# Embedding, attention, state and sign layers for 64 sequences on one core: xn1's turn ahead of the key projection

## The chip, the cores and the metric

The program runs on one core of a Trainium2 chip. The metric is the device time in microseconds (us) of one execution. Of the kernel before there are three timed runs and one profiled execution.

## The reference, cut to what matters

For 64 sequences of 128 token ids, each with 256 features:

```python
x = emb[inp]                                   # [64, 128, 256]
q, k, v = x @ Wq.T + bq, x @ Wk.T + bk, x @ Wv.T + bv     # 16 heads of 16
attn = softmax(q k^T / 4); h = (attn v) @ Wo.T + bo
n = layernorm(h)
gate = sigmoid(n @ gate_w.T + gate_b)
state = exclusive_scan(decay, (n @ B_w.T) @ C_w.T)        # over the 128 tokens
h = h + gate * state
h = h + layernorm(h) @ sign(weight).T
```

## The kernel before, in words

Two sequences make a pair, so there are 32 pairs. The function `turns` runs 38 turns, t from -2 to 35; a hardware loop holds those from 6 to 29. A turn is a software pipeline: in turn t the attention of pair t is computed, the queries and keys of pair t + 1 are made, and the rest of the layer runs for pairs t - 1 to t - 4. Each engine has its own `turn` function, in which the order of its instructions is written out by hand; semaphores order the engines among each other (`await_event`), and no scheduler moves anything.

The attention of a pair has 8 steps, s = 0 to 7, four heads of one sequence each. In TensorE's `attention(s)` (L730) stand:

- `turn_probs(s)`: four transposes of the probabilities of step s - 2 into `ps_t` (L695);
- `scores(s)`: two products into `ps_s` (L683);
- `context(s)`: eight narrow products of step s - 3 into the bank `ps_c` (L712). For s = 3 this is step 0 of pair t, and it waits until ScalarE has moved the second half of pair t - 1 out of `ps_c` (`move_ctx`, L357, tile `ctx_raw`).

All of TensorE's products share line 623, and all copies through `move_block` on ScalarE share L364, so the tiles tell them apart. A projection is made of float32 operands split in a high and a low part: ScalarE casts the high part out of a PSUM bank (`xTh`, `xn1Th`), VectorE subtracts it from the same bank for the low part (`xTl`, `xn1Tl`, L494, `low_features`), and TensorE multiplies high by high, high by low and low by high.

Around the change a turn goes so:

- TensorE after `attention(2)`: the prefix sums of pair t - 3 (`earlier` by `state_in` into bank g3, L753), the transposes of the embeddings of pair t + 1 into g0 (`to_features`, L758, tile `x_emb`), `attention(3)`, the context rows of pair t - 1 into g2 (L720), the key projection of pair t + 1 into g1 (L766, 12 products), which waits for `xTl`, and the transposes of the normed `xn1` of pair t - 2 into g3 (L770), which wait until the bank g3 has been read.
- ScalarE in steps 2 and 3: `move_probsT(2)` (L347), the copy `xTh` (L374), the copy `ctx_raw` (L375), the exponentials of step 2 (L338), `move_probsT(3)`, the exponentials of step 3.
- VectorE in step 2: the maxima of the scores (L486), `v_aug` (L567), `xTl` (L572), the two halves of `xn1` (`norm_apply`, L519), `gated` (L578), which reads the sums out of g3, and `h1` (L583), which adds `h0`.

GpSimd issues the gathers of the embeddings (L277) and computes the inverse square roots of the layer norms (L286, L291). SyncE spreads keys and queries over partitions with 12 transfers per pair, into `k_stack` and `q_stack`, which the scores of the next turn read.

Of the kernel before, what the change touches and what calls it, by code (L numbers as in the profile page):

```python
# [52 lines left out]
def build(nc, x, emb, wqT, bq, wkT, bk, wvT, bv, woT, bo, b_w, c_wT, gate_wT, gate_b, log_decay, ffn_wT, out):  # L53
    ctx = ExitStack()
    with ctx:
# [60 lines left out]
        xn1, xn2 = sb("xn1", [P, 2, D]), sb("xn2", [P, 2, D])  # L116
# [55 lines left out]
        def exists(pair):  # L172

            return not isinstance(pair, int) or 0 <= pair < PAIRS

        def await_event(eng, semaphore, per, pair, nth):

            if exists(pair):
                eng.wait_ge(semaphore, pair * per + nth)
# [120 lines left out]
        def _(act):  # L300
# [29 lines left out]
            def turn(t, par):  # L330
                def exponentials(s):

                    if exists(t):
                        await_event(act, dve_max, STEPS, t, s + 1)
                        p2, s2 = before(t, s, 2)
                        await_event(act, pe_pT, STEPS, p2, s2 + 1)
                        for j in range(HPS):
                            last = nc.scalar.activation(probs[s % 2][:, j], ps_s[s % 2][:, j * SEQ:j * SEQ + SEQ],  # L338
                                                        ACT.Exp, bias=neg_max[s % 2][:, j:j + 1])
                        last.then_inc(act_exp, 1)  # L340
# [18 lines left out]
                def move_block(pair, dst, src, filled, freed, done):  # L359

                    if exists(pair):
                        await_event(act, filled, 1, pair, 1)
                        await_event(act, freed, 1, pair - 1, 1)
                        nc.scalar.copy(dst[:], src[:]).then_inc(done, 1)  # L364
# [6 lines left out]
                exponentials(1)  # L371

                move_probsT(2)
                move_block(t + 1, xT[0], g0, pe_x, pe_v, act_x)  # L374
                move_ctx(t - 1, 1)  # L375
                exponentials(2)

                move_probsT(3)
                exponentials(3)
# [39 lines left out]
        def _(dve):  # L419
# [59 lines left out]
            def turn(t, par):  # L479
# [84 lines left out]
                if exists(t):  # L564
# [4 lines left out]
                        g2[:].rearrange("p (b h w) -> p b h w", b=2, w=HD),  # L569
                        bv_row[:].rearrange("p (h w) -> p h w", w=HD).unsqueeze(1).to_broadcast([P, 2, HEADS, HD]),  # L570
                        ALU.add).then_inc(dve_v, 1)
                low_features(t + 1, xT, g0, act_x, pe_v, dve_xlo)  # L572
                if exists(t - 2):
                    norm_apply(t - 2, h0[par], mv1, rs1, xn1, rs1_done, pe_xn1T, dve_xn1)
                if exists(t - 3):
                    await_event(dve, pe_sums, 1, t - 3, 1)
                    await_event(dve, act_tanh, 1, t - 3, 1)
                    nc.vector.scalar_tensor_tensor(gated[:], gate_tanh[:], 1.0,  # L578
                                                   g3[:].rearrange("p (b d) -> p b d", b=2), ALU.add,
                                                   ALU.mult).then_inc(dve_gated, 1)  # L580
                    await_event(dve, dve_gated, 1, t - 3, 1)
                    await_event(dve, dve_y, 1, t - 4, 1)
                    nc.vector.tensor_tensor(h1[:], gated[:], h0[1 - par][:], ALU.add).then_inc(dve_h1, 1)  # L583
# [37 lines left out]
        def _(pe):  # L621
# [53 lines left out]
            def turn(t, par):  # L675
# [84 lines left out]
                if exists(t - 1):  # L760
                    await_first((dve_v, 1, t, 1), (dve_h0, 1, t - 2, 1))
                    context_rows(1, g2)
                if exists(t + 1):
                    await_event(pe, dve_xlo, 1, t + 1, 1)
                    await_first((dve_ctx, 2, t - 1, 1), (dve_klo, C, t, C))
                    feature_major(g1, wk, xT, pe_k)  # L766
                if exists(t - 2):
                    await_event(pe, dve_xn1, 2, t - 2, 2)
                    await_event(pe, dve_h1, 1, t - 3, 1)
                    to_features(g3, lambda b: xn1[:, b], pe_xn1T)  # L770

                attention(4)
                if exists(t + 1):
# [59 lines left out]
```

## Time and profile before

| | us |
|---|---|
| median of 3 runs | 828.27 |
| lowest, highest | 826.53, 829.21 |
| the profiled execution | 829.6 |
| its span | 827.5 |
| TensorE busy, weight loads | 755.6, 644.6 |
| VectorE busy | 584.8 |
| ScalarE busy | 582.0 |
| GpSimd busy | 130.5 |

The profiled execution is 1.3 us above the median. Busy times of TensorE overlap in part, since its products are pipelined; what it does in a stretch is read from the starts of its instructions. The mean granted clock of TensorE is 0.98 of full speed; it is below it in the first and the last few slices alone.

### The profile page before, as it was taken

What the parts mean: (1) busy time and instruction counts of PE and PEld (TensorE: products, weight loads), DVE (VectorE), ACT (ScalarE), POOL (GpSimd) and SP (SyncE); (2) the same over time, 40 slices, a digit from 0 to 9 for tenths busy, and PEclk for the clock granted to TensorE, in tenths of its full rate; (3) what the DMA queues carried; (4) which work ended last, traced back from release to release, by engine and by line L of the source; (5) the groups of instructions that cost most, each with busy time, mean ns of one, the idle gap of its engine ahead of it and who ended that gap; (6) DMA issues with size and microseconds to landing.
All of it is one profiled execution on the core that took longest, in us unless ns stands there. A gap on an engine that the chain in (4) does not pass through costs nothing.

```text
span 827.5 us, 21122 instructions
## 1 busy us (share of the span) xinstructions
PE 755.6 (91%) x7047; PEld 644.6 (78%) x7047; DVE 584.8 (71%) x1307; ACT 582.0 (70%) x1643; POOL 130.5 (16%) x205
## 2 busy tenths in 40 slices
PE   1389999999999999999999999999999999999964
PEld 0377888888888888888888888888888888888754
DVE  5345677777777777777777787777777777777763
ACT  2177877777777777777777777777877777778710
POOL 7210111111110111111101111111011111100010
PEclk9889999999999999999999999999999999999986
DMA  4222223123322321233223322332233222322000
GB/s 129 89 90 78 90 91 97 52 85 103 100 91 89 101 94 59 75 101 101 89 89 101 101 56 73 98 101 90 88 101 101 61 73 94 101 90 90 15 14 25
DMA packets 56015, 69.67 MB, mean 84 GB/s; under 512 B 6768, under 2 KB 41648, under 8 KB 55984
## 3 DMA queue, kind: packets, MB, share of 16 engines
q1 hardware_dynamic: 52048, 60.48, 21.3%
q0 software_dynamic: 3072, 8.39, 4.9%
q10 hardware_dynamic: 864, 0.40, 0.2%
q8 instruction: 18, 0.29, 0.2%
q14 instruction: 13, 0.11, 0.0%
HBM read 10.52 MB, written 8.39 MB: 23 GB/s over the span
## 4 chain that ended last, share of the span: by engine, by line
PE 76%; issue 13%; ACT 3%; DVE 2%; DMA 2%; SPq 2%; POOL 1%; ACTq 1%; POOLq 0%; DVEq 0%
PE ps_g L623 39%; PE ps_t L695 11%; PE ps_c L623 10%; PE ps_g L672 7%; PE ps_s L623 6%; PE ps_g L720 4%; ACT ctx_raw L357 2%; SPq L234 1%; DMA q_stack<-q_low 1%; DVE raw L452 1%; DMA gb_row<-in_gate_b 1%; SPq L239 0%; POOL rs L286 0%; DMA raw<-in_woT 0%; POOL rs L291 0%
## 5 line engine op out<-in xcount | busy, mean ns | idle before, releaser
L338 ACT ACTIVATE probs<-ps_s,neg_max 128x128 f32<-128x128 f32 x1024 | 299.6, 400 | 73.0 <-DVE neg_max L486 72.9
L486 DVE TENSOR_REDUCE neg_max<-ps_s 128x4 f32<-128x512 f32 x256 | 176.4, 689 | 155.2 <-PE ps_s L623 132.7
L347 ACT COPY probsT<-ps_t 128x512 f32<-128x512 f32 x256 | 155.5, 608 | 63.7 <-PE ps_t L695 54.2
L695 PE MATMUL ps_t<-ident,probs 128*128 128x128 f32 x1024 | 154.7, 274 | 3.9 <-ACT probsT L347 3.9
L623 PE MATMUL ps_s<-k_stack,q_stack 128*128 128x256 f32 x512 | 124.2, 325 | 7.8 <-DMA q_stack<-q_low 7.8
L623 PE MATMUL ps_c<-probsT,v_aug 128*32 128x128 f32 x2048 | 109.3, 285 | 16.6 <-ACT ctx_raw L357 16.1
L695 PEld LDWEIGHTS ps_t<-ident,probs 128*128 128x128 f32 x1024 | 120.0, 142 | 5.6 <-ACT probs L338 3.3
L286 POOL TENSOR_TENSOR rs<-ve,neg_half 128x2 f32<-128x2 f32 x32 | 22.2, 693 | 449.4 <-DVE ve L513 449.4
L623 PEld LDWEIGHTS ps_s<-k_stack,q_stack 128*128 128x128 f32 x512 | 78.1, 193 | 8.8 <-DMA q_stack<-q_low 8.7
L623 PEld LDWEIGHTS ps_c<-probsT,v_aug 128*32 128x32 f32 x2048 | 40.5, 108 | 53.3 <-ACT ctx_raw L357 17.5
L277 POOL DMA_INDIRECT x_emb<-in_emb,id_col x64 | 64.5, 1008 | 37.5 <-PE ps_g L672 21.7
L364 ACT CAST xTh<-ps_g 128x512 fp32r<-128x512 f32 x32 | 18.8, 586 | 56.0 <-PE ps_g L672 56.0
L291 POOL TENSOR_TENSOR rs<-ve,neg_half 128x2 f32<-128x2 f32 x32 | 22.8, 714 | 197.7 <-DVE ve L513 197.7
L501 DVE BATCH_NORM_STATS2 stats<-h 128x6 f32<-128x256 f32 x128 | 47.9, 416 | 1.2
L672 PE MATMUL ps_g<-ident,xn 128*128 128x128 f32 x256 | 39.6, 278 | 9.4 <-DVE h L583 5.0
L494 DVE TENSOR_TENSOR xTl<-ps_g,xTh 128x512 fp32r<-128x512 f32 x32 | 22.2, 693 | 36.5 <-ACT xTh L364 36.5
L519 DVE TENSOR_SCALAR xn<-h,mv,rs 128x256 f32<-128x256 f32 x128 | 46.6, 406 | 1.8 <-POOL rs L286 1.0
L623 PE MATMUL ps_g<-wgh,xn1Th 128*128 128x256 f32 x128 | 39.8, 311 | 1.4 <-DVE xn1Tl L494 1.4
L623 PE MATMUL ps_g<-xTh,wkh 128*128 128x256 f32 x128 | 39.3, 307 | 1.7 <-DVE xTl L494 1.7
L720 PE MATMUL ps_g<-ident,ctx_raw 128*128 128x128 f32 x256 | 40.4, 281 | 0.0
L623 PE MATMUL ps_g<-wvh,xTh 128*128 128x256 f32 x128 | 40.0, 312 | 0.0
L623 PE MATMUL ps_g<-wsh,xn1Th 128*128 128x256 f32 x128 | 39.7, 310 | 0.0
(120 smaller groups left out, 1829.1 us busy)
## 6 DMA issues: line engine op xcount, KB each, us to landing
k_stack<-k_high SPq DMA_DIRECT2D x128, 128.0 KB, 2.4
q_stack<-q_high SPq DMA_DIRECT2D x64, 256.0 KB, 2.5
k_stack<-k_low SPq DMA_DIRECT2D x64, 128.0 KB, 2.3
q_stack<-q_low SPq DMA_DIRECT2D x32, 256.0 KB, 2.5
out<-y SPq DMA_DIRECT2D x32, 256.0 KB
x_emb<-in_emb,id_col POOLq DMA_INDIRECT x64, 3.6
raw<-in_wkT SPq DMA_DIRECT2D x1, 256.0 KB, 3.1
raw<-in_wqT SPq DMA_DIRECT2D x1, 256.0 KB, 4.2
```

What stands on the lines that cost most here:

```text
L277: nc.gpsimd.indirect_dma_start(x_emb[par][b][:], None, emb, bass.IndirectOffsetOnAxis(ap=id_col[par][b][:], axis=0)).then_inc(gathered[par ...
L286: nc.gpsimd.tensor_tensor(rs1[:], ve1[:], neg_half[:], ALU.pow).then_inc(rs1_done, 1)
L291: nc.gpsimd.tensor_tensor(rs2[:], ve2[:], neg_half[:], ALU.pow).then_inc(rs2_done, 1)
L338: last = nc.scalar.activation(probs[s % 2][:, j], ps_s[s % 2][:, j * SEQ:j * SEQ + SEQ], ACT.Exp, bias=neg_max[s % 2][:, j:j + 1])
L347: nc.scalar.copy(probsT[st % 2][:], ps_t[:]).then_inc(act_pT, 1)
L486: nc.vector.tensor_reduce(neg_max[s % 2][:], ps_s[s % 2][:].rearrange("p (h k) -> p h k", h=HPS), axis=AX.X, op=ALU.max, negate=True).then ...
L501: nc.vector.bn_stats(stats[:, b], h[:, b]).then_inc(done_st, 1)
L519: nc.vector.tensor_scalar(xn[:, b], h[:, b], mv[:, b, 0:1], rs[:, b:b + 1], ALU.subtract, ALU.mult).then_inc(done, 1)
L623: return nc.tensor.matmul(dst, lhsT, rhs, start=first, stop=last)
L672: last = nc.tensor.transpose(dst[:, at:at + SEQ], src(b)[:, c * P:c * P + P], ident[:])
L695: last = nc.tensor.transpose(ps_t[:, j * SEQ:j * SEQ + SEQ], probs[st % 2][:, j], ident[:])
L720: last = nc.tensor.transpose(dst[:, g * P:g * P + P], ctx_raw[b][:, g], ident[:])
```

## The change

Three engines get another order in steps 2 and 3, and one wait becomes another:

- ScalarE copies the contexts and computes the exponentials of step 2 before it copies the embeddings.
- VectorE forms `xn1` and `gated` before it forms `xTl`; `h1` follows `xTl`.
- TensorE turns `xn1` before the key projection, and waits there for `gated` in place of `h1`.

The diff:

```diff
@@ ScalarE
                 move_probsT(2)
-                move_block(t + 1, xT[0], g0, pe_x, pe_v, act_x)
                 move_ctx(t - 1, 1)
                 exponentials(2)
+                move_block(t + 1, xT[0], g0, pe_x, pe_v, act_x)
@@ VectorE
-                low_features(t + 1, xT, g0, act_x, pe_v, dve_xlo)
                 if exists(t - 2):
                     norm_apply(t - 2, h0[par], mv1, rs1, xn1, rs1_done, pe_xn1T, dve_xn1)
                 if exists(t - 3):
...
                     nc.vector.scalar_tensor_tensor(gated[:], gate_tanh[:], 1.0,
                                                    g3[:].rearrange("p (b d) -> p b d", b=2), ALU.add,
                                                    ALU.mult).then_inc(dve_gated, 1)
+                low_features(t + 1, xT, g0, act_x, pe_v, dve_xlo)
+                if exists(t - 3):
                     await_event(dve, dve_gated, 1, t - 3, 1)
                     await_event(dve, dve_y, 1, t - 4, 1)
                     nc.vector.tensor_tensor(h1[:], gated[:], h0[1 - par][:], ALU.add).then_inc(dve_h1, 1)
@@ TensorE
                     context_rows(1, g2)
+                if exists(t - 2):
+                    await_event(pe, dve_xn1, 2, t - 2, 2)
+                    await_event(pe, dve_gated, 1, t - 3, 1)
+                    to_features(g3, lambda b: xn1[:, b], pe_xn1T)
                 if exists(t + 1):
                     await_event(pe, dve_xlo, 1, t + 1, 1)
                     await_first((dve_ctx, 2, t - 1, 1), (dve_klo, C, t, C))
                     feature_major(g1, wk, xT, pe_k)
-                if exists(t - 2):
-                    await_event(pe, dve_xn1, 2, t - 2, 2)
-                    await_event(pe, dve_h1, 1, t - 3, 1)
-                    to_features(g3, lambda b: xn1[:, b], pe_xn1T)
```

ScalarE in the middle of a turn of the filled pipeline, before: `probsT` is `move_probsT`, `probs` the exponentials, `xTh` the high part of the embeddings.

```order
L347 COPY probsT<-ps_t 128x512
L364 CAST xTh<-ps_g 128x512
L357 COPY ctx_raw<-ps_c 128x512
L338 ACTIVATE probs<-ps_s,neg_max 128x128 x4
L347 COPY probsT<-ps_t 128x512
```

And now, in the same place:

```order
L347 COPY probsT<-ps_t 128x512
L357 COPY ctx_raw<-ps_c 128x512
L338 ACTIVATE probs<-ps_s,neg_max 128x128 x4
L364 CAST xTh<-ps_g 128x512
L347 COPY probsT<-ps_t 128x512
```

The copy of the contexts no longer stands behind the copy of the embeddings, and that copy stands behind four exponentials more.

VectorE in step 2 and at the start of step 3 of such a turn, before; `neg_max` is the maxima, the `h` behind `gated` is `h1`.

```order
L494 TENSOR_TENSOR xTl<-ps_g,xTh 128x512
L519 TENSOR_SCALAR xn<-h,mv,rs 128x256 x2
L578 SCALAR_TENSOR_TENSOR gated<-gate_tanh,ps_g 128x512
L583 TENSOR_TENSOR h<-gated,h 128x512
L179 REGISTER_ALU
L486 TENSOR_REDUCE neg_max<-ps_s 128x4
```

And now (one line more stands in the file from here on, so L583 has become L584); the two halves of `xn` stand right ahead of this piece:

```order
L577 SCALAR_TENSOR_TENSOR gated<-gate_tanh,ps_g 128x512
L179 REGISTER_ALU
L494 TENSOR_TENSOR xTl<-ps_g,xTh 128x512
L584 TENSOR_TENSOR h<-gated,h 128x512
L179 REGISTER_ALU
L486 TENSOR_REDUCE neg_max<-ps_s 128x4
```

`xTl` has moved behind three instructions that do not need it, and its place ahead of `h1` and the maxima is kept.

## Rows read from the trace of the kernel before

**Rows 1.** The page, part 1: busy time, share of the span and instructions by engine.

```profile
PE 755.6 (91%) x7047; PEld 644.6 (78%) x7047; DVE 584.8 (71%) x1307; ACT 582.0 (70%) x1643; POOL 130.5 (16%) x205
```

**Rows 2.** Who waited for whom: us in total, times, longest us.

```profile
PE ps_c L623 <- ACT ctx_raw L357: 16.1, 30, 0.6
```

**Rows 3.** Timeline, TensorE, one turn: start, us, instruction, idle before and its releaser.

```profile
412.56 0.43 PE L623 MATMUL ps_c<-probsT,v_aug 128*32 128x128 f32 x8
412.92 1.12 PE L623 MATMUL ps_g<-state_in,earlier 128*128 128x512 f32 x2
413.88 0.60 PE L672 MATMUL ps_g<-ident,x_emb 128*128 128x128 f32 x4
...
414.68 0.48 PE L623 MATMUL ps_s<-k_stack,q_stack 128*128 128x256 f32 x2
415.72 0.42 PE L623 MATMUL ps_c<-probsT,v_aug 128*32 128x128 f32 x8 [0.56 <-ACT ctx_raw L357]
416.08 0.66 PE L720 MATMUL ps_g<-ident,ctx_raw 128*128 128x128 f32 x4
416.49 0.36 PE L623 MATMUL ps_g<-xTh,wkh 128*128 128x256 f32 x1
...
418.01 0.63 PE L672 MATMUL ps_g<-ident,xn 128*128 128x128 f32 x4
418.48 0.60 PE L695 MATMUL ps_t<-ident,probs 128*128 128x128 f32 x4
```

**Rows 4.** Timeline, ScalarE, the same turn.

```profile
414.59 0.59 ACT L364 CAST xTh<-ps_g 128x512 fp32r<-128x512 f32 x1 [1.57 <-PE ps_g L672]
415.07 0.59 ACT L357 COPY ctx_raw<-ps_c 128x512 f32<-128x512 f32 x1
415.55 1.16 ACT L338 ACTIVATE probs<-ps_s,neg_max 128x128 f32<-128x128 f32 x4
416.56 0.63 ACT L347 COPY probsT<-ps_t 128x512 f32<-128x512 f32 x1
```

**Rows 5.** Timeline, VectorE, the same turn.

```profile
412.67 0.69 DVE L486 TENSOR_REDUCE neg_max<-ps_s 128x4 f32<-128x512 f32 x1 [0.85 <-ACT probs L338]
413.28 0.68 DVE L567 TENSOR_TENSOR v_aug<-ps_g,bv_row 128x512 f32<-128x512 f32 x1
415.21 0.69 DVE L494 TENSOR_TENSOR xTl<-ps_g,xTh 128x512 fp32r<-128x512 f32 x1 [1.25 <-ACT xTh L364]
415.82 0.73 DVE L519 TENSOR_SCALAR xn<-h,mv,rs 128x256 f32<-128x256 f32 x2
416.46 0.68 DVE L578 SCALAR_TENSOR_TENSOR gated<-gate_tanh,ps_g 128x512 f32<-128x512 f32 x1
...
417.78 0.68 DVE L486 TENSOR_REDUCE neg_max<-ps_s 128x4 f32<-128x512 f32 x1
```

**Rows 6.** Timeline, TensorE, turn 31, the last with an attention: scores and context of step 3.

```profile
767.92 0.48 PE L623 MATMUL ps_s<-k_stack,q_stack 128*128 128x256 f32 x2
768.33 0.43 PE L623 MATMUL ps_c<-probsT,v_aug 128*32 128x128 f32 x8
```

**Rows 7.** Timeline, turn 0 on VectorE and TensorE, and the start of turn 1's scores.

```profile
45.44 0.69 DVE L486 TENSOR_REDUCE neg_max<-ps_s 128x4 f32<-128x512 f32 x1 [2.98 <-PE ps_s L623]
...
47.66 0.39 PE L623 MATMUL ps_g<-xTh,wkh 128*128 128x256 f32 x1 [0.19 <-DVE xTl L494]
...
59.01 0.50 PE L623 MATMUL ps_s<-k_stack,q_stack 128*128 128x256 f32 x2 [0.91 <-DMA q_stack<-q_low]
```

**Rows 8.** Timeline, GpSimd, the turn of rows 3: the second gather's issue.

```profile
413.55 0.95 POOL L277 DMA_INDIRECT x_emb<-in_emb,id_col  x1 [0.30 <-issue]
```

**Rows 9.** The turn's last transfer to a stack, its landing (page, part 6), the next scores.

```profile
426.57 0.61 SPq L239 DMA_DIRECT2D q_stack<-q_low  x1
...
q_stack<-q_low SPq DMA_DIRECT2D x32, 256.0 KB, 2.5
...
430.50 0.48 PE L623 MATMUL ps_s<-k_stack,q_stack 128*128 128x256 f32 x2
```

## The prediction

> **What bounds the kernel now.** I read the page first, then who waited for whom, then the timelines of one turn, engine by engine. The page shows TensorE busy for 91% of the span and VectorE and ScalarE for 71% and 70% [rows 1]. So TensorE is the engine to follow, and a change of order that adds and removes no instruction can only win what TensorE waits. In the filled pipeline the view of waits has one wait of TensorE that comes back: its context products wait for the copy `ctx_raw`, 30 times, 16.1 us in total, never over 0.6 us [rows 2]. There are 30 turns in which both that copy and the copy of the embeddings exist, turns 1 to 30.
>
> The timeline says why. ScalarE waits 1.57 us with the copy `xTh` until TensorE has turned the embeddings, and the copy `ctx_raw`, which needs only products that ended at 412.99, stands in the queue behind it: it starts at 415.07 and TensorE goes on at 415.72 [rows 3, 4]. The exponentials of step 2 stand there too; their maxima were ready at 413.36 [rows 5], they start at 415.55.
>
> How much is the wait worth? Its row says 0.56 us of idle time. Starts say more: from the scores of step 3 to their context products it is 1.04 us here [rows 3]. Turn 31 has no embeddings to copy and so is a turn of this kernel without that block: there it is 0.41 us [rows 6]. I take the difference, **0.63 us** per turn, because TensorE's time is the distance of starts. The idle time of the waits' row, 16.1 / 30 = 0.54 us, is the low bound.
>
> **The change, part by part.** I lay the new order over the turn of rows 3 to 5, on its own clock.
>
> *ScalarE.* The copy `ctx_raw` can start when the context products of step 2 have ended, 412.99, say 413.06. A copy takes its place for 0.48 us (415.07 to 415.55) and four exponentials for 1.01 us (415.55 to 416.56) [rows 4]. So the exponentials start at 413.54, behind maxima that ended at 413.36, and ScalarE is free at 414.55. The transposes of the embeddings end at 414.48, and `xTh` started 0.11 us later, at 414.59 [rows 3, 4]. It starts at 414.59 again: the four exponentials just fit in what was idle time, with 0.04 us to spare. This is the tightest fit of the sum, though nothing is lost at once if it fails (below).
>
> *VectorE.* After `v_aug` (start 413.28) the next place is 413.88 with the distance of 0.61 us that follows such an instruction (415.21 to 415.82). `xn` goes there and takes 0.64 us, `gated` starts at 414.52. It needs the prefix sums, whose products end at 414.04 [rows 3], and ends at 415.20. `xTl` needs `xTh`, which ends at 415.18, and starts at 415.21 as before, ending at 415.90. `h1` at 415.82 and the maxima of step 3 at 416.43 follow, the latter 1.35 us earlier than now [rows 5].
>
> *TensorE.* Context products of step 3 at 414.68 + 0.41 = 415.09 (`ctx_raw` has ended at 413.65), context rows at 415.45, the turn of `xn` at 415.86, with the distances of 0.36 and 0.41 us in rows 3. It needs `gated`: ended at 415.20, 0.66 us to spare. Had the wait stayed on `h1` (416.51) it would have cost 0.7 us; this is what the new wait is for. The turn takes 0.47 us, so the key projection starts at 416.33 and needs `xTl`: ended at 415.90, 0.43 us to spare. It takes 1.52 us (416.49 to 418.01), and step 4 begins at 417.85 in place of 418.48 [rows 3]. Nothing of the 0.63 us is lost here. The move of the projection behind the transposes costs nothing by itself, as the same groups stand there with the same lengths.
>
> *What is late next.* Behind step 4 everything that ScalarE and VectorE do is released by TensorE or by the maxima of step 3, which move by 1.35 us, so all keeps its distance to TensorE or gains. The transfers: the last one for the stack is issued at 426.57 and lands 2.5 us later, at 429.07; the scores that need it start at 430.50 [rows 9]. That is 1.43 us of cover, and 0.80 us are left even if no transfer moves. SyncE's queue keeps its order, and it starts behind the high part of the keys, which comes earlier. GpSimd gets nothing new.
>
> *The turns that do not profit.* Before turn 3 there are no prefix sums. They fill 0.96 us (412.92 to 413.88) [rows 3], and it is in these that the exponentials of step 2 find room. Count from the start of the context products of step 2. Without sums the old order has the embeddings' transposes at +0.36, `xTh` at +1.07, `ctx_raw` at +1.55, step 3's context products at +2.20 and the key projection at +2.97. The new one has `ctx_raw` at +0.50, exponentials at +0.98, `xTh` at +1.99, `xTl` at +2.61 to +3.30, and the projection at +3.34. Turn 1 loses 0.37 us. In turn 2 the turn of `xn`, 0.47 us, moves ahead and fills the gap: it gains 0.10 us. In turn 0 there is no `ctx_raw`: the maxima of step 2 end at 46.13, the exponentials leave at 47.18, `xTl` ends at 48.49, and the projection starts at 48.53 in place of 47.66 [rows 7]. These 0.87 us go on through the keys and the transfers to the scores of turn 1, which already wait for the stack. In the last turns TensorE waits for a chain through VectorE in which nothing moves; I put them at zero, within 0.2 us.
>
> **The sum:** turns 3 to 30 win 28 x 0.63 = 17.6 us, turn 2 0.1; turns 0 and 1 cost 0.87 + 0.37 = 1.2. That is **-16.5 us**. Against the profiled execution's own 829.6 it gives 813.1; that execution is 1.3 us above the median of the runs, and against the median, 828.27, it gives **811.8 us**. By the low bound (28 x 0.54, less 1.1) it would be -14.0 and 814.3; by the longest idle time of that row, 0.6, with the 0.07 on top that starts show over idle time here, it is 28 x 0.67 - 1.1 = 17.7, and 810.6. With 1.4 us for the spread of three runs the forecast's own range is 809.2 to 815.7.
>
> **The rivals.**
>
> *VectorE and GpSimd get in each other's way.* `xn` moves from 415.82 to 413.88, into the issue of the second gather, which runs from 413.55 to 414.50 [rows 8]. If `xn` had to wait for its end, it would start at 414.50, `gated` at 415.14, `xTl` at 415.75 and end at 416.44. The projection would start at 416.48, 0.15 us late, and a turn would win 0.48 us: 28 x 0.48 - 1.1 = 12.3, or **816.0 us**. Against it: two `xn` of 256 elements take 0.64 us and one `v_aug` of 512 takes 0.61 us [rows 5], so `xn` shows no faster way of reading that could need more ports than `v_aug` does. The Trainium skill, in "SBUF — State Buffer", section "Who interferes with whom", states that VectorE and GpSimd share one pair of ports, that a tensor_scalar in a two-port mode takes it for its whole length, and that whichever comes second is blocked; `xn` is a tensor_scalar. By that rule, were `xn` in such a mode, the time would be the 816 of this rival; outside it the page sees no conflict. Chance 0.08.
>
> *Another wait takes the gap.* The stack's landing is the nearest: 1.43 us of cover, of which the gain takes 0.63. If the transfers landed 1.4 us later than the row's 2.5, the whole gain would become a wait for `q_stack`, and the time would stay at **828**. Against it: the transfers begin earlier than now. That the change is without effect, for the queues being in truth in another order, is as good as excluded, as the orders above are written out by hand. Together 0.06.
>
> *Slower: the exponentials in front of the copy of the embeddings.* The place is ScalarE at 414.55. If they leave later than 415.02, the key projection waits for `xTl`; from 415.65 on (1.06 us late: 0.43 to spare and the 0.63 won) the turn is longer than before, since also keys, transfers and step 4 wait. Turns 0 and 1 show that this can happen. If all turns lost what turn 1 loses, it would be 28 x 0.37 + 1.1 = 11.5 us more, **839.8 us**. For it: only 0.04 us between the two. Against it: it takes a full us, and what precedes (maxima at 412.67, context products at 412.56) is released by TensorE itself in each turn. Chance 0.06.
>
> **How the numbers follow.** The forecast has 0.80, the ports 0.08, no gain 0.06, slower 0.06. Faster by over 0.3% (2.5 us, about what a measurement of this kernel can tell from no change) are the first two, 0.88; within it 0.06; slower 0.06. The range reaches from the forecast's low end, 809.2, to the ports' case and 1 us of spread, 817.0.
>
> **What the profile after should show.** The wait of `ps_c` for `ctx_raw` is gone from the list, and the distance from the scores to the context products of step 3 is 0.41 us in all turns. `ctx_raw` starts about 0.5 us behind the context products of step 2, the exponentials next, `xTh` right at the end of the embeddings' transposes. A turn is 0.63 us shorter than before. TensorE does not wait for `gated`, and for `xTl` only in turns 0 to 2. `xn` still takes 0.64 us and starts 0.6 us behind `v_aug`. A row of TensorE waiting for `xTl` in every turn would speak for the ports if `xn` starts late, and for the last rival if `xTh` does; a row for `q_stack` in every turn for the other. Were the distance 0.41 and the turn still as long, my reading of the turn would be wrong.

## The result, and the profile after

The changed kernel took **808.64 us** (median of four runs, 808.38 to 809.01), beside 828.24 us for the kernel before (826.53 to 829.21). The ratio is 0.9766, with a 95% interval of 0.9749 to 0.9783. It was timed twice more, beside other experiments: 810.33 us each time, with 827.82 and 827.43 us for the kernel before, ratios 0.9792 (0.9773 to 0.9810) and 0.9791 (0.9773 to 0.9809). So the gain is 17 to 20 us. The forecast was 811.8 us, a gain of 16.5; the first measurement lies 0.6 us below the low end of its range, 809.2, and the other two lie inside it.

The page, part 1, of the kernel after. Instructions and busy times have hardly changed [rows 1]; the span is 20.7 us shorter than 827.5.

```profile
span 806.8 us, 21122 instructions
...
PE 750.4 (93%) x7047; PEld 642.4 (80%) x7047; DVE 579.7 (72%) x1307; ACT 585.7 (73%) x1643; POOL 129.2 (16%) x205
```

Who waited for whom, TensorE of the kernel after (us in total, times, longest us). The wait of [rows 2] is not in the list any more. `gated` and `xTl` are waited for at the pipeline's two ends alone: for the stretch from 100 to 742 us this view has no wait of TensorE at all.

```profile
PE ps_s L624 <- DMA q_stack<-q_low: 7.6, 2, 6.7
...
PE ps_g L624 <- DVE xTl L494: 3.8, 4, 1.5
...
PE ps_g L673 <- DVE gated L577: 3.1, 2, 2.7
```

Timeline of the kernel after, TensorE, one turn, to be laid beside [rows 3]: start, us, instruction. The next turn's prefix sums start at 424.92.

```profile
401.98 1.13 PE L624 MATMUL ps_g<-state_in,earlier 128*128 128x512 f32 x2
402.94 0.60 PE L673 MATMUL ps_g<-ident,x_emb 128*128 128x128 f32 x4
...
403.74 0.48 PE L624 MATMUL ps_s<-k_stack,q_stack 128*128 128x256 f32 x2
404.14 0.43 PE L624 MATMUL ps_c<-probsT,v_aug 128*32 128x128 f32 x8
404.50 0.66 PE L721 MATMUL ps_g<-ident,ctx_raw 128*128 128x128 f32 x4
405.00 0.60 PE L673 MATMUL ps_g<-ident,xn 128*128 128x128 f32 x4
405.35 0.37 PE L624 MATMUL ps_g<-xTh,wkh 128*128 128x256 f32 x1
```

From scores to context products it is 0.40 us instead of 1.04, and a turn is 22.94 us long; before it was 23.54 and 23.61 in turn.

Timelines of ScalarE and VectorE of the kernel after, the same turn [rows 4, 5].

```profile
402.21 0.58 ACT L357 COPY ctx_raw<-ps_c 128x512 f32<-128x512 f32 x1
402.69 1.15 ACT L338 ACTIVATE probs<-ps_s,neg_max 128x128 f32<-128x128 f32 x4
403.70 0.61 ACT L364 CAST xTh<-ps_g 128x512 fp32r<-128x512 f32 x1
404.17 0.63 ACT L347 COPY probsT<-ps_t 128x512 f32<-128x512 f32 x1
```

```profile
402.34 0.68 DVE L567 TENSOR_TENSOR v_aug<-ps_g,bv_row 128x512 f32<-128x512 f32 x1
402.94 0.74 DVE L519 TENSOR_SCALAR xn<-h,mv,rs 128x256 f32<-128x256 f32 x2
403.59 0.67 DVE L577 SCALAR_TENSOR_TENSOR gated<-gate_tanh,ps_g 128x512 f32<-128x512 f32 x1
404.34 0.69 DVE L494 TENSOR_TENSOR xTl<-ps_g,xTh 128x512 fp32r<-128x512 f32 x1
404.95 0.68 DVE L584 TENSOR_TENSOR h<-gated,h 128x512 f32<-128x512 f32 x1
405.55 0.69 DVE L486 TENSOR_REDUCE neg_max<-ps_s 128x4 f32<-128x512 f32 x1
```

Each piece stands where the prediction put it: the four exponentials between `ctx_raw` and `xTh`, `xTh` 0.76 us behind the start of the embeddings' transposes (0.71 before), `gated` ended at 404.26 for a turn of `xn` at 405.00 (0.74 to spare), `xTl` ended at 405.03 for a projection at 405.35 (0.32 to spare).

The difference of the two spans, split at starts of TensorE's groups (the sums of turn 3 start at 105.81 before and at 103.68 after, those of turn 31 at 766.60 and 746.13):

| stretch | before | after | difference | forecast |
|---|---|---|---|---|
| to the first `x_emb` transposes | 26.10 | 25.24 | -0.86 | 0 |
| from there to turn 3's sums | 79.71 | 78.44 | -1.27 | +1.14 |
| turns 3 to 30 | 660.79 | 642.45 | -18.34 | -17.64 |
| turn 31's sums to the end | 60.90 | 60.67 | -0.23 | 0 |
| span | 827.5 | 806.8 | -20.7 | -16.5 |

Against the forecast the start is off by 2.4 us, the filled turns by 0.7. The 0.86 us of the first row lie ahead of all that the change touches. The last row looks right and is not: in two more profiles of the changed kernel this stretch takes 59.25 and 59.27 us, as is shown below.

The filled turns win 0.60 or 0.67 us each, 0.635 in the mean, as the sum had it. Most of the rest is one turn. Turn 5, the last one ahead of the hardware loop, waited for its first scores in the kernel before, which I had not seen. TensorE's timeline there, before:

```profile
146.70 0.60 PE L695 MATMUL ps_t<-ident,probs 128*128 128x128 f32 x4
147.49 0.50 PE L623 MATMUL ps_s<-k_stack,q_stack 128*128 128x256 f32 x2 [0.19 <-DMA q_stack<-q_low]
```

These scores start 0.79 us behind the transposes ahead of them; elsewhere it is 0.35 us. From the sums of turn 4 to those of turn 5 it took 24.07 us. In the kernel after, the same distance is 22.99 us, beside 22.94 in a steady turn, and no wait is left there. The cause is one transfer. The last transfer of turn 4 to `q_stack` was issued at 143.08, 3.97 us ahead of the place at which the scores could start, as in a steady turn (3.93) [rows 9], but it took 4.4 us to land, the longest of all transfers to `q_stack`. The view of the tile `q_stack`, before:

```profile
DMA to landing us min/median/max: 2.4/2.5/4.4
```

After the change the transfer of that turn is issued 4.61 us ahead of the scores and lands in 2.6 us. Why it lands late in the one and not in the other the traces do not say. That is a gain of 0.44 us that the sum lacks; the remaining 0.26 us are 0.01 us per turn.

The start: from the embeddings' transposes to the key projection of turns 0 and 1 it was 2.46 and 2.68 us before and is 3.32 and 3.02 after, so +0.86 and +0.34 us for a forecast of +0.87 and +0.37. For turn 0 this agreement is luck, as the next section shows. What hid the loss is TensorE's clock. Busy times in the stretch 60 to 64 us of the kernel before (us, then PE, PEld, DVE, ACT, POOL busy with their counts, the granted clock, DMA share, GB/s):

```profile
60.00:64.00 4.00, 4.00 (x27) 3.39 (x26) 1.52 (x4) 2.87 (x9) 0.00 (x0) 0.57 0.01 2
```

The same stretch of the kernel after:

```profile
60.00:64.00 4.00, 4.00 (x45) 3.34 (x43) 2.39 (x5) 3.41 (x10) 0.00 (x0) 1.00 0.00 0
```

In the one, the clock is near its lower level (0.5 is 1.2 GHz of 2.4) and TensorE has 27 instructions in 4 us; in the other it is at full speed and they are 45. Ahead of it, from 52 to 60 us, TensorE was busy for 5.1 us of 8 in both. Whether it falls in this place is not a property of the order alone, as the next section shows.

### The profile page after: what moved, and what is told of

It is laid out like the page before. It is cut to its first block, busy times and chain, and to the rows that moved or that the text cites. A ratio compares the mean times of both kernels' runs of the same rounds, so it can differ in the third digit from the quotient of the medians.

```text
span 806.8 us, 21122 instructions
## 1 busy us (share of the span) xinstructions
PE 750.4 (93%) x7047; PEld 642.4 (80%) x7047; DVE 579.7 (72%) x1307; ACT 585.7 (73%) x1643; POOL 129.2 (16%) x205
## 4 chain that ended last, share of the span: by engine, by line
PE 80%; issue 12%; DVE 2%; DMA 2%; ACT 1%; SPq 1%; POOL 1%; ACTq 0%; POOLq 0%; DVEq 0%
PE ps_g L624 41%; PE ps_t L696 12%; PE ps_c L624 10%; PE ps_s L624 7%; PE ps_g L673 6%; PE ps_g L721 4%; SPq L234 1%; DMA gb_row<-in_gate_b 1%; DMA q_stack<-q_low 1%; DVE raw L452 1%; DMA raw<-in_woT 0%; POOL rs L286 0%; ACT probs L338 0%; POOL rs L291 0%; DVE xTl L494 0%
## 5 line engine op out<-in xcount | busy, mean ns | idle before, releaser
L338 ACT ACTIVATE probs<-ps_s,neg_max 128x128 f32<-128x128 f32 x1024 | 295.1, 383 | 79.7 <-DVE neg_max L486 79.3
L347 ACT COPY probsT<-ps_t 128x512 f32<-128x512 f32 x256 | 153.1, 598 | 75.6 <-PE ps_t L696 74.6
L357 ACT COPY ctx_raw<-ps_c 128x512 f32<-128x512 f32 x64 | 38.3, 598 | 3.6 <-PE ps_c L624 0.5
L624 PE MATMUL ps_g<-xTh,wqh 128*128 128x256 f32 x128 | 39.7, 310 | 0.0
```

The lines of the kernel that those rows point to most:

```text
L347: nc.scalar.copy(probsT[st % 2][:], ps_t[:]).then_inc(act_pT, 1)
L357: nc.scalar.copy(ctx_raw[b][:], ps_c[:]).then_inc(act_ctx, 1)
L624: return nc.tensor.matmul(dst, lhsT, rhs, start=first, stop=last)
```

## The experiments

All times stand beside runs of the kernel before in the same set: 827.82 us for the first set (kernel after again, before again, two kinds of early turns), 827.47 for the second (parts alone), 827.43 for the third. "Turn" is the distance of the prefix sums of two turns in the filled pipeline, "start" the distance from the first embeddings' transposes to turn 3's sums. Each expectation says which theories it sets against each other.

### The early turns, and the spread of the start

**The changed kernel unaltered, once more.**

> The changed kernel unaltered, for another profile of its start. If the lower clock at the start falls at a random place, the distances between the embeddings' transposes of turns -1, 0 and 1 differ from the first profile's 18.21 and 19.69 us by up to 2 us; if it belongs to the order of the work, they repeat within 0.1. Time 808.6 either way.

Measured: 810.33 us (808.96 to 812.11). Turn 22.94, as at first. The distances named there are 18.60 and 21.98 us in place of 18.21 and 19.69, so the lower clock does not belong to the order of the work alone. The start is 81.11 us, where it was 78.44 in the first profile of the same kernel. Its stretch from 60 to 64 us:

```profile
60.00:64.00 4.00, 4.00 (x30) 3.15 (x23) 1.74 (x4) 2.31 (x8) 0.00 (x0) 0.50 0.01 2
```

So the changed kernel can have the low clock there as well.

**The kernel before unaltered, once more.**

> The kernel before unaltered, for another profile of its start and of turn 6. If the half clock from 60 to 64 us and the wait of turn 6's scores for the query stack (0.44 us between starts) belong to the old order, both come again; if they are chance, at least one is gone. Time 828.2.

Measured: 827.6 us (825.52 to 829.19). Start 77.41 (79.71 in the first profile), and this is the same stretch:

```profile
60.00:64.00 4.00, 3.75 (x36) 3.21 (x35) 2.36 (x6) 2.86 (x8) 0.00 (x0) 1.00 0.01 4
```

The clock in the start differs between two executions of one kernel, in either order. The long turn stays in part, 23.84 us beside 23.6 from turn 4's sums to turn 5's (the expectation's "turn 6" is this turn 5): the transfer ahead of it lands in 4.1 us. With this profile as the kernel before, turns 3 to 30 take 660.46 us and the change wins 18.02 there.

With both starts at full clock in this stretch, 78.44 after and 77.41 before, the change costs 1.03 us there; the forecast was 1.14. The match is partly chance. The forecast for turn 0 was read from a profile in which that turn's transposes ran at the lower clock (granted 0.69 from 44 to 48 us). TensorE's timeline there, in the first profile of the kernel before:

```profile
45.20 1.05 PE L672 MATMUL ps_g<-ident,x_emb 128*128 128x128 f32 x4
```

And in this one:

```profile
43.70 0.60 PE L672 MATMUL ps_g<-ident,x_emb 128*128 128x128 f32 x4
```

Here the key projection follows their start by 2.14 us in place of 2.46. So at the full clock turn 0 loses 3.32 - 2.14 = 1.18 us to the new order, 0.31 more than forecast. From turn 0's transposes to turn 3's sums it is 58.95 us here and 60.23 in the first profile after, 1.28 more; the other 0.25 us between this and 1.03 lie ahead of these transposes.

**The end of the pipeline.** The profiles of these two runs show one thing more. From turn 31's sums to the end the kernel before takes 60.90 and 60.89 us in two profiles; the changed kernel takes 60.67, 59.25 and 59.27 in three. In turns 32 and 33 TensorE waits with the turn of `xn1` until VectorE is done, before for `h1`, now for `gated`. TensorE's timelines in turn 33, of the first profile before and of this second profile after:

```profile
803.42 0.63 PE L672 MATMUL ps_g<-ident,xn 128*128 128x128 f32 x4 [3.42 <-DVE h L583]
805.45 0.58 PE L623 MATMUL ps_g<-wgh,xn1Th 128*128 128x256 f32 x1 [1.40 <-DVE xn1Tl L494]
```

```profile
785.27 0.63 PE L673 MATMUL ps_g<-ident,xn 128*128 128x128 f32 x4 [2.70 <-DVE gated L577]
787.85 0.58 PE L624 MATMUL ps_g<-wgh,xn1Th 128*128 128x256 f32 x1 [1.95 <-DVE xn1Tl L494]
```

The wait is 0.72 us shorter, as it is in turn 32 (0.73), and the new event does it: in turn 32 the turn of `xn1` stands 20.96 us behind turn 31's sums with ScalarE's old order and the wait for `gated` (826.05 us, below), and 21.68 with all of the change but the wait for `h1` kept (837.71 us, below), as in the kernel before. But the next wait, for the low part of `xn1`, is 0.55 longer, and by these products only 0.25 us are left of the whole gain. The larger part of the 1.6 us is the clock. Busy times from 38 to 44 us behind turn 31's sums, in the same two profiles:

```profile
804.60:810.60 6.00, 5.15 (x24) 5.15 (x25) 1.44 (x4) 0.67 (x2) 0.69 (x1) 0.50 0.01 3
```

```profile
787.25:793.25 6.00, 5.31 (x30) 5.07 (x30) 1.77 (x4) 0.65 (x2) 0.69 (x1) 0.72 0.01 3
```

From the gate's products of turn 33 to the turn of `xn2` it takes 5.69 us in the one and 4.71 in the other, and 0.43 us come on top by the end, again at a lower clock before. In the first profile after, it is the clock too that takes most of the gain: it was 0.50 from 24 to 30 us behind turn 31's sums, and by the turn of `xn2` in turn 32 1.1 us were lost against the second.

**The old order of ScalarE for t < 3 alone.**

```diff
                 move_probsT(2)
+                early = isinstance(t, int) and t < 3
+                if early:
+                    move_block(t + 1, xT[0], g0, pe_x, pe_v, act_x)
                 move_ctx(t - 1, 1)
                 exponentials(2)
-                move_block(t + 1, xT[0], g0, pe_x, pe_v, act_x)
+                if not early:
+                    move_block(t + 1, xT[0], g0, pe_x, pe_v, act_x)
```

> The changed kernel, but in turns before turn 3 ScalarE copies the embeddings ahead of the contexts and the exponentials, as before. Theory A (the new ScalarE order costs time in the turns without prefix sums: 0.87 us in turn 0, 0.37 in turn 1, 0.10 less in turn 2): about 1.1 us faster than the changed kernel, 807.5 us, and from the embeddings' transposes to the key projection turn 0 takes 2.5 us in place of 3.3. Theory B (what was missing in my sum is that the start of the new order is not worse but better, through what it triggers): slower than the changed kernel by up to 2 us.

Measured: 808.6 us (806.19 to 808.95), ratio 0.9765 (0.9747 to 0.9783), 1.7 us below the changed kernel in the same set. Transposes to projection in turns 0 to 2: 2.14, 2.68, 3.11 us, where the changed kernel has 3.33, 3.01, 3.02. The loss of turns 0 and 1 is the exponentials' place, as A says, and turn 0 loses more than A had (2.14 us for an expected 2.5). The time alone would not show it: the intervals of the two ratios overlap by 0.001.

**Contexts, embeddings, exponentials, in all turns.** The old order had the embeddings first, the new one has the exponentials in the middle; this has neither.

```diff
                 move_ctx(t - 1, 1)
-                exponentials(2)
                 move_block(t + 1, xT[0], g0, pe_x, pe_v, act_x)
+                exponentials(2)
```

> The changed kernel, but ScalarE's order in step 2 is contexts, embeddings, exponentials. Theory A (only the copy of the contexts has to move ahead; the exponentials find room either way): the steady turn stays at 22.94 us and turns 0 to 2 lose nothing: 807.5 us. Rival: the exponentials of step 2, 1.5 us later than in the changed kernel, are late for the probabilities' transposes of step 4 or push the keys back into the stack's wait: a turn over 23.0 us and 810 us or more.

Measured: **807.09 us** (803.51 to 808.71), ratio 0.9746 (0.9724 to 0.9769). Turn 22.94, the same as with the exponentials first. The gain lies in turns 0 to 2, where the projection follows the transposes by 2.14, 2.05 and 2.47 us. Turn 0, TensorE of the changed kernel:

```profile
43.45 0.60 PE L673 MATMUL ps_g<-ident,x_emb 128*128 128x128 f32 x4
...
46.77 0.39 PE L624 MATMUL ps_g<-xTh,wkh 128*128 128x256 f32 x1 [1.26 <-DVE xTl L494]
```

And of this one:

```profile
43.48 0.60 PE L673 MATMUL ps_g<-ident,x_emb 128*128 128x128 f32 x4
...
45.62 0.39 PE L624 MATMUL ps_g<-xTh,wkh 128*128 128x256 f32 x1
```

**The same kernel and the changed one again, side by side.**

> The version with contexts, embeddings, exponentials on ScalarE once more, beside the changed kernel in the same job. Theory A (its turns 0 to 2 lose nothing to the order): 1 to 3 us faster than the changed kernel run beside it, embeddings' transposes to key projection of turn 0 at 2.1 us in place of 3.3 at the full clock. Rival: the difference of the first job was chance in the clock of the start: within 1 us.

> The changed kernel unaltered, beside the version above. 808.4 to 811 us; a steady turn of 22.94 us; no late start of xTh behind the exponentials in any turn.

Measured: 807.31 us (806.3 to 807.48; 0.9756, 0.9741 to 0.9772) against 810.33 (808.8 to 811.41; 0.9791, 0.9773 to 0.9809). Twice the difference is 3.0 to 3.2 us with intervals that do not overlap, so this order beats both kernels. Starts in the profiles: 78.37 and 81.44 us. Of these 3.1 us, the three distances from transposes to projection account for 2.6 (2.19, 2.06 and 2.47 here, 6.72 together, against 3.32, 3.02 and 3.02, 9.36); what else is in it, clock or transfers, was not separated.

### Which part brings the gain

**ScalarE's part without the rest.** The kernel before, with the new order on ScalarE alone.

```diff
                 move_probsT(2)
-                move_block(t + 1, xT[0], g0, pe_x, pe_v, act_x)
                 move_ctx(t - 1, 1)
                 exponentials(2)
+                move_block(t + 1, xT[0], g0, pe_x, pe_v, act_x)
```

> The kernel before with ScalarE's part of the change alone. My theory (the 0.63 us are freed at the context products, but VectorE's old order keeps h1 at its old place, and TensorE's turn of xn1 waits for it): TensorE waits for h1 in place of ctx_raw, step 4 begins at most 0.1 us earlier in a turn, 28 turns give under 3 us and the start costs 1: about 826 us, a turn of 23.45 to 23.55 us. Rival (the copy ctx_raw alone was the price): a turn of 22.94 us and 810 us.

Measured: 836.07 us (835.18 to 837.71), ratio 1.0110 (1.0092 to 1.0129). Both theories missed the time, though mine had the wait right: the one for `ctx_raw` is gone, but a turn is 23.69 us, and 9 of the 24 turns in the hardware loop take 24.0 to 24.1. From turn 3's sums to turn 4's it is 25.00 us, with a wait of 1.14 us for the transfer to `q_stack` in it. In the list of waits of TensorE stand in its place:

```profile
PE ps_g L672 <- DVE h L583: 15.4, 31, 3.4
...
PE ps_g L623 <- DVE xTl L494: 6.9, 13, 1.5
```

TensorE waits for `h1` every turn, since VectorE still begins with `xTl` and brings `h1` out last of four. One turn of it on TensorE, from the projection's last products to the turn of `xn`, and VectorE's `h1`:

```profile
420.65 0.28 PE L623 MATMUL ps_g<-xTh,wkl 128*128 128x256 f32 x1
421.31 0.63 PE L672 MATMUL ps_g<-ident,xn 128*128 128x128 f32 x4 [0.38 <-DVE h L583]
```

```profile
420.47 0.69 DVE L583 TENSOR_TENSOR h<-gated,h 128x512 f32<-128x512 f32 x1
```

So the copy's new place alone moves the 0.6 us from one wait to another and adds some.

**The rest without ScalarE's part.** The changed kernel with the two lines of ScalarE back in their old order.

```diff
                 move_probsT(2)
+                move_block(t + 1, xT[0], g0, pe_x, pe_v, act_x)
                 move_ctx(t - 1, 1)
                 exponentials(2)
-                move_block(t + 1, xT[0], g0, pe_x, pe_v, act_x)
```

> The changed kernel with ScalarE's old order, so VectorE's and TensorE's parts alone. My theory (ScalarE's order is what frees TensorE): the wait for ctx_raw stays at 0.63 us between starts, a turn stays at 23.57 us, 828 us within 1.5. Rival (the orders on VectorE and TensorE bring time by themselves, by an earlier start of the maxima of step 3): a turn under 23.4 us.

Measured: 826.05 us (823.22 to 828.44), ratio 0.9979 (0.9962 to 0.9995). Turn 23.50 and 23.57, and the old wait is there:

```profile
PE ps_c L624 <- ACT ctx_raw L357: 16.2, 30, 0.6
```

VectorE's and TensorE's parts alone bring 1.4 us, with an interval below 1. In its profile turns 3 to 30 take 659.39 us, 1.1 to 1.4 less than in the two of the kernel before, and the end takes 59.38 us, 1.5 less.

**TensorE waits for `h1` again, all else as changed.**

```diff
                     await_event(pe, dve_xn1, 2, t - 2, 2)
-                    await_event(pe, dve_gated, 1, t - 3, 1)
+                    await_event(pe, dve_h1, 1, t - 3, 1)
                     to_features(g3, lambda b: xn1[:, b], pe_xn1T)
```

> The changed kernel, but TensorE waits for h1 ahead of the turn of xn1, as before. In the changed kernel's trace h1 ends at 405.64 and TensorE comes to that place at 405.00. My theory: every turn from 3 on loses 0.65 to 0.7 us, 28 of them 18 to 19.6 us, and the time is back at 827 to 829 us, with a wait of TensorE for h1 in every turn. Rival (there is slack behind it, since the keys do not set the turn): under 815 us.

Measured: 837.71 us (836.93 to 838.25), ratio 1.0124 (1.0107 to 1.0141), 9 to 11 us more than expected. The wait has the size that was worked out: the turn of `xn` follows the context rows by 1.28 us where the changed kernel has 0.50, 0.78 us more for a forecast of 0.7.

```profile
418.34 0.66 PE L721 MATMUL ps_g<-ident,ctx_raw 128*128 128x128 f32 x4
419.62 0.63 PE L673 MATMUL ps_g<-ident,xn 128*128 128x128 f32 x4 [0.62 <-DVE h L584]
```

Such a turn takes 23.73 us, 0.79 more than 22.94, which is 2.5 to 4 us over 28 turns above what was expected. 13 of the 24 turns in the hardware loop take 24.1 to 24.2 us instead, some 5 us more, and in those `xTh` starts late. That was a new finding, taken up below.

**The key projection ahead of the turn of `xn`.** The changed kernel with TensorE's old order, but the wait for `gated` kept.

```diff
-                if exists(t - 2):
-                    await_event(pe, dve_xn1, 2, t - 2, 2)
-                    await_event(pe, dve_gated, 1, t - 3, 1)
-                    to_features(g3, lambda b: xn1[:, b], pe_xn1T)
                 if exists(t + 1):
...
                     feature_major(g1, wk, xT, pe_k)
+                if exists(t - 2):
+                    await_event(pe, dve_xn1, 2, t - 2, 2)
+                    await_event(pe, dve_gated, 1, t - 3, 1)
+                    to_features(g3, lambda b: xn1[:, b], pe_xn1T)
```

> The changed kernel, but TensorE keeps the key projection ahead of the turn of xn1 (which still waits for gated alone). In the changed kernel's trace xTl ends at 405.03 and TensorE would come to the projection at 404.91. My theory: 0.16 us lost per turn, from turn 3 on 4.5 us, and 0.3 to 0.5 us in turn 2: about 814 us, a turn of 23.1 us. Rival (the transposes' place is of no weight): 809 to 810 us and 22.94. Rival (xn1 turned late delays the gate's operands): over 816 us.

Measured: 821.75 us (818.66 to 824.03), ratio 0.9921 (0.9898 to 0.9944). Good turns take 23.11 to 23.14 us, as my theory said, but 17 of the 24 in the hardware loop take 23.5 to 23.6. So the time is above the 816 us of the last rival, though nothing in the trace is the rival's cause. The two kinds differ in ScalarE. A good one, then the next, from ScalarE's timeline:

```profile
410.90 1.15 ACT L338 ACTIVATE probs<-ps_s,neg_max 128x128 f32<-128x128 f32 x4
411.91 0.61 ACT L364 CAST xTh<-ps_g 128x512 fp32r<-128x512 f32 x1
...
434.03 1.15 ACT L338 ACTIVATE probs<-ps_s,neg_max 128x128 f32<-128x128 f32 x4
435.45 0.59 ACT L364 CAST xTh<-ps_g 128x512 fp32r<-128x512 f32 x1 [0.28 <-PE ps_g L673]
```

And the embeddings' transposes on which it waits, with the projection that waits for its low part:

```profile
411.16 0.60 PE L673 MATMUL ps_g<-ident,x_emb 128*128 128x128 f32 x4
...
434.30 0.60 PE L673 MATMUL ps_g<-ident,x_emb 128*128 128x128 f32 x4
...
436.81 0.39 PE L624 MATMUL ps_g<-xTh,wkh 128*128 128x256 f32 x1 [0.30 <-DVE xTl L494]
```

In both turns ScalarE comes to the copy about 1.01 us behind the exponentials' start and 0.74 to 0.75 behind the transposes' start. In the first it begins at once; in the second it begins 0.41 us later, 1.15 behind the transposes, and the projection is late.

### What the late start of `xTh` hangs on

**Both: key projection first, and the embeddings' copy ahead of the exponentials.** The last kernel's TensorE with the ScalarE order of the 807 us kernel.

> Two edits on the changed kernel: the key projection ahead of the turn of xn1 on TensorE, and contexts, embeddings, exponentials on ScalarE. With the first edit alone, about half of the turns had xTh start 1.15 us behind the embeddings' transposes in place of 0.75, and took 23.5 us in place of 23.1. Theory A (the late starts come from the copy's place right behind the exponentials, at which its release arrives just then): no late start here, all turns at 23.1 us or less, about 811 us. Theory B (the transposes themselves end late in such turns, or the order on TensorE does it): about half of the turns at 23.5 us again, 817 us or more.

Measured: 810.7 us (809.25 to 812.07), ratio 0.9806 (0.9785 to 0.9826), 11 us below the same TensorE order with the exponentials in front (its set had 827.47 for the kernel before, this one 827.43). Turns 22.96 to 23.12, none late; `xTh` starts 0.63 to 0.71 us behind the transposes in each, as before the change, with idle time ahead of it:

```profile
402.68 0.58 ACT L364 CAST xTh<-ps_g 128x512 fp32r<-128x512 f32 x1 [0.86 <-PE ps_g L673]
```

So late starts were seen only where the copy stands right behind the exponentials and its release falls close to their end. They were seen only in turns of the hardware loop too, 39 of 72 in the three kernels, and in none of the turns 3, 4, 5 and 30, whose instructions stand outside it and where `xTh` follows by 0.66 to 0.67 us. What in the loop does it stays open.

**The embeddings' copy one place later still,** behind `move_probsT(3)`: the rival that `xTh` is what decides, doubled.

```diff
                 exponentials(2)
-                move_block(t + 1, xT[0], g0, pe_x, pe_v, act_x)

                 move_probsT(3)
+                move_block(t + 1, xT[0], g0, pe_x, pe_v, act_x)
                 exponentials(3)
```

> The changed kernel, but ScalarE copies the embeddings one place later still, behind the copy of the probabilities of step 3. In the changed kernel's trace xTh would start 0.8 us later (404.50 in place of 403.70), xTl end at 405.80, and TensorE come to the key projection at 405.35. My theory (0.3 us to spare, the rest is lost one to one): 0.49 us per turn, a turn of 23.4 us; with the start about 823 to 825 us, and TensorE waits for xTl in every turn. Rival (no slack): 0.8 us per turn, 833 us. Rival (the projection is not on the path): 809 to 811.

Measured: 827.13 us (824.35 to 828.09), ratio 0.9989 (0.9977 to 1.0002). Turn 23.47 for an expected 23.4, and the wait that the prediction named for a late `xTh`, every turn:

```profile
PE ps_g L624 <- DVE xTl L494: 12.9, 32, 1.8
```

The start takes 83.75 us, 2.3 more than the longest of the changed kernel's three, and the time is above the expected 823 to 825. Here `xTh` starts 1.55 to 1.56 us behind the transposes, 0.8 later than in the changed kernel, and the turn is 0.53 longer, as 0.8 less the 0.32 us that `xTl` had to spare gives 0.5. The margins of the projection are as the trace shows them, and one copy set 0.8 us too late takes back the whole gain.

## Where the prediction was right, and which steps failed

**The wait is what bounded the kernel: right.** With ScalarE's part it goes, and without it 826.05 us are left. A turn won 0.60 to 0.67 us for 0.63, and 0.40 us between scores and context products is what turn 31 had shown [rows 6].

**ScalarE's order needs the wait for `gated`: right, and stronger than I said.** "Had the wait stayed on `h1` it would have cost 0.7 us" measured 0.78. ScalarE's order alone costs 8.6 us. TensorE's new order is needed less: with the projection first 5.7 us are won, but 16.7 with the projection first and the embeddings' copy ahead of the exponentials.

**Turns 0 and 1: right in kind, turn 0 by luck in size.** +0.86 and +0.34 us for +0.87 and +0.37. But rows 7 show a turn 0 at the lower clock; against one at the full clock it is +1.18.

**The margins.** `gated` had 0.74 us to spare for a forecast 0.66; `xTl` 0.32 for 0.43. Counted from the prefix sums, `xTl` ends at +3.05 us where my lay-out had +2.98, and the projection starts at +3.37 for +3.41; the turn of `xn` starts 0.50 us behind the context rows and not 0.41, but the projection follows it by 0.35 and not 0.47.

**Ports: refuted for this place.** `xn` started at 402.94, 0.60 us behind `v_aug`, and its two halves took 0.65 us (402.94 to 403.59) while the gather was being issued, as GpSimd's timeline of the kernel after shows:

```profile
402.61 0.94 POOL L277 DMA_INDIRECT x_emb<-in_emb,id_col  x1 [0.31 <-issue]
```

The same pair took 0.64 us with no issue beside it [rows 5]. The issue itself took 0.94 us, for 0.95 [rows 8]. The Trainium skill, "SBUF — State Buffer", section "Who interferes with whom", states that a tensor_scalar in a two-port mode and GpSimd shut each other out, and that the later of the two is blocked; here that would be `xn`, which starts 0.33 us behind the issue. This case shows no such exclusion, which fits the page if `xn` is in no such mode.

**What failed: the last turns were put at zero.** The prediction says: "In the last turns TensorE waits for a chain through VectorE in which nothing moves; I put them at zero, within 0.2 us." The end won 1.6 us in two of three profiles (60.9 against 59.25 and 59.27), and 0.2 in the first. The chain stands still, but the change moves the place in it for which TensorE waits, from the end of `h1` to that of `gated`: two waits of 1.16 and 3.42 us became 0.43 and 2.70. As the next wait grew, this brought 0.25 us. The other 1.4 are stretches at the lower clock that became shorter, for which the sum has no term. Why they do is not shown; they came alike in both profiles before, and alike in the second and the third after.

**What failed: the filled turns and the transfer.** "turns 3 to 30 win 28 x 0.63 = 17.6 us" measured 18.34, and 18.02 with the other profile of the kernel before. I had set the cover of a steady turn, 1.43 us, against the median landing of 2.5 us [rows 9], but in turn 4 the transfer landed in 4.4 and 4.1 us, and the kernel before paid for it. The terms for the end and for the filled turns together were 2.0 to 2.3 us too small; less the 0.3 us that turn 0 costs beyond its forecast, the sum would have given about 810. The rest down to 808.64 is within the spread.

**What failed: the spread.** "With 1.4 us for the spread of three runs" was too little: the start alone came out between 78.44 and 81.44 us in three profiles of the changed kernel, as the clock fell in another place, and the end differs by 1.4 us. The three profiled spans are 806.8, 808.5 and 808.9 us. In the first measurement all four runs were at the quick end (808.4 to 809.0); the ten runs of the other two lie at 808.8 to 812.1. Against these the forecast is 1.5 us too high, 0.6 to 1.0 of it in the gain over the kernel before beside them. Why the first four agree among themselves stays open.

**The slower side was nearer than I wrote.** Of the 0.04 us between the exponentials' end and the copy's release I said that "nothing is lost at once if it fails". The kernel with the key projection first shows a loss of 0.4 us in 17 of 24 turns with just this fit. In the changed kernel it did not occur in the filled turns of any of three profiles: in the hardware loop `xTh` follows the transposes by 0.74 to 0.77 us in all. Why the same ScalarE program starts late in three of the other kernels and never in this one I could not tell; the trace shows the same instructions ahead of it with the same lengths. By an estimate from these numbers a late start there would cost 0.09 us a turn, 0.41 less the 0.32 that `xTl` has to spare.

## What to carry to other kernels

A copy that stands behind a late copy in an engine's queue can be the whole bound though neither is long; put first what is ready first, and read on the engine that waits what comes due next, since here ScalarE's move without the new wait and VectorE's order turned a gain of 17 us into a loss of 9. Where two orders give the same filled turn, take the one in which the copy with the latest release does not stand behind a long group: it was 3 us better here, most of it at the pipeline's start, and no turn was late in any kernel with that order. And read margins in the filling and the emptying turns too, not in a steady one alone, and a transfer's longest landing beside its median: where the engine that is followed waits much, at both ends of the pipeline, stretches of lower clock lay elsewhere from profile to profile, and were worth 1 to 3 us here.

## What the hardware showed unexpectedly

The granted clock at the start falls in different places in executions of one kernel: 0.57, 1.00 (before), 1.00, 0.50 (after) in the stretch from 60 to 64 us, each time behind 8 us of which TensorE was busy for 5.1 to 5.6. With it the start of one kernel varies by 2.3 us (before, two profiles) and 3.0 us (after, three profiles); its runs differ by 3 to 4 us. A change of 0.3% at the start can't be read from single profiles here.

An instruction whose release comes just ahead of its turn in the queue can start at once or some 0.4 us later, turn by turn, with nothing else different that the trace shows. In three kernels 9, 13 and 17 of the 24 turns of the hardware loop were late, and no turn outside it; in the changed kernel, with the same instructions on ScalarE, none was, nor in the kernels with idle time of 0.8 us ahead of the same copy.

One transfer, the last to `q_stack` in turn 4, took 4.4 and 4.1 us to land in two profiles of the kernel before, where the median is 2.5, and 2.6 and 2.7 in the changed kernel.
